# Second half of a two-layer transformer on one core: routed pass stored in tile order, rows gathered by the tokens, attention interleaved with the gathers

## The reference

```python
x = x + 0.5 * _L0_ffn_ref(_layernorm(x), ...)     # 8 experts, all computed, weighted
x = x + _L0_attn_ref(_layernorm(x), ...)          # landmark attention
x = x + 0.5 * _L0_ffn_ref(_layernorm(x), ...)
x = x + 0.5 * _L1_ffn_ref(_layernorm(x), ...)     # "first routed pass"
x = x + _L1_attn_ref(_layernorm(x), ...)          # window attention, "second attention"
x = x + 0.5 * _L1_ffn_ref(_layernorm(x), ...)     # "second routed pass"
```

```python
def _L1_ffn_ref(x, router_w, router_bias, gate_w, up_w, down_w, sgate_w, sup_w, sdown_w):
    scores = softmax(flat @ router_w.T + router_bias)          # 32 experts
    topk_scores, topk_idx = top_k(scores, 4); topk_scores /= topk_scores.sum()
    h = silu(flat @ gate_w[e].T) * (flat @ up_w[e].T)          # of the 4 chosen experts
    out = sum over the 4 of topk_scores * (h @ down_w[e].T)
    out = out + silu(flat @ sgate_w.T) * (flat @ sup_w.T) @ sdown_w.T   # shared expert
def _L1_attn_ref(x, ...):
    # q, k, v projections; 7 windows of 128 tokens, 64 apart, in each batch of 512;
    # scores/sqrt(8), softmax over the window, @ v; overlapping windows averaged; @ Wo + bo
```

## Time and profile before

| | us |
|---|---|
| three runs | 958.69, 956.48, 963.06 (median 958.69) |
| the profiled execution | 960.52 |
| its span in the trace | 959.3 |
| PE / DVE / ACT / POOL busy | 750.2 / 566.3 / 426.3 / 495.5 |
| indirect DMAs of the two tile loops on POOL (190) | 181.9 busy |
| dispatches on POOL (128) | 128.1 busy |

### The profile page before, as it was taken

How to read it: one execution, slowest core, us unless ns; L and a number is a source line. 1 busy time by engine, 2 the same in 40 slices (tenths; PEclk the granted TensorE clock), 3 DMA queues, 4 the chain that set the end, 5 groups by cost and what they waited for, 6 DMA issues and landing times.

```text
span 959.3 us, 18763 instructions
## 1 busy us (share of the span) xinstructions
PE 750.2 (78%) x6298; PEld 619.6 (65%) x6298; DVE 566.3 (59%) x1726; ACT 426.3 (44%) x1110; POOL 495.5 (52%) x488
## 2 busy tenths in 40 slices
PE   6889888999999997988977667626766896767750
PEld 5778655589777766777766656624566775666640
DVE  6975576668677588877743343318667663333325
ACT  3567646556155454555214555521532222555440
POOL 4656620036280055357753777754147770777773
PEclk9999979999799999999997999976965798999995
DMA  9999999700230050011123344333001112334316
GB/s 226 218 216 216 212 213 219 159 4 4 71 107 1 1 154 1 13 37 49 52 62 83 105 111 107 92 107 140 1 25 51 55 58 67 107 105 112 104 60 224
DMA packets 125758, 94.74 MB, mean 99 GB/s; under 512 B 10496, under 2 KB 116480, under 8 KB 125664
## 3 DMA queue, kind: packets, MB, share of 16 engines
q1 hardware_dynamic: 113472, 71.19, 32.0%
q0 software_dynamic: 10176, 21.65, 6.7%
q10 hardware_dynamic: 2016, 0.69, 0.3%
HBM read 34.12 MB, written 59.38 MB: 97 GB/s over the span
## 4 chain that ended last, share of the span: by engine, by line
PE 48%; DVE 22%; ACT 9%; POOL 9%; issue 8%; DMA 3%; SPq 1%; ACTq 0%; DVEq 0%; POOLq 0%
POOL sorted_rows L445 6%; PE banks L1625 5%; ACT y L704 5%; PE banks L793 5%; PE banks L774 4%; DVE t_low L722 3%; PE banks L1097 3%; PE banks L1654 3%; PE banks L1672 3%; PE banks L775 3%; PE banks L776 2%; ACT t_high L681 2%; PE banks L394 2%; PE banks L396 2%; PE banks L395 2%
## 5 line engine op out<-in xcount | busy, mean ns | idle before, releaser
L674 POOL DMA_INDIRECT expert_rows<-y,goal x190 | 181.9, 957 | 105.1 <-issue 60.9
L445 POOL DMA_INDIRECT sorted_rows<-rows_x,row_of x128 | 128.1, 1000 | 68.7 <-issue 36.9
L774 PE MATMUL banks<-routed_high,t_high 128*128 x192 | 60.5, 315 | 65.3 <-DVE t_low L722 65.3
L977 ACT ACTIVATE ys<-banks,wtab 128x128 f32<-128x128 f32 x256 | 73.0, 369 | 66.0 <-PE banks L1097 55.8
L774 PEld LDWEIGHTS banks<-routed_high,t_high 128*128 128x128 f32 x192 | 37.6, 196 | 76.8 <-issue 76.8
L394 PE MATMUL banks<-x_high,w_high 128*128 128x512 f32 x192 | 86.3, 450 | 0.4 <-POOL w_low L867 0.4
L739 DVE TENSOR_TENSOR h<-sg,banks 128x512 f32<-128x512 f32 x48 | 33.0, 687 | 88.8 <-ACT sg L688 88.8
L1097 PE MATMUL banks<-w,hT 128*128 128x128 f32 x512 | 72.5, 286 | 15.2 <-DVE hT L1018 14.9
L1097 PEld LDWEIGHTS banks<-w,hT 128*128 128x128 f32 x512 | 66.2, 196 | 24.1 <-DVE hT L1018 21.7
L902 POOL TENSOR_TENSOR x<-ys,x 128x512 f32<-128x512 f32 x44 | 56.3, 1280 | 46.4 <-ACT ys L977 45.8
L396 PE MATMUL banks<-x_high,w_low 128*128 128x512 f32 x192 | 77.8, 405 | 0.0
(11 more groups left out here) (297 smaller groups left out, 1911.4 us busy)
## 6 DMA issues: line engine op xcount, KB each, us to landing
sorted_rows<-zeros SPq DMA_DIRECT2D x32, 1120.0 KB, 17.3
tile<-sorted_rows SPq DMA_DIRECT2D x192, 70.0 KB
routed_low<-in_ffn_w SPq DMA_DIRECT2D x8, 512.0 KB, 3.8
w<-in_ffn_w SPq DMA_DIRECT2D x20, 192.0 KB, 4.0
expert_rows<-y,goal POOLq DMA_INDIRECT x190, 2.3
routed_down<-in_ffn_w SPq DMA_DIRECT2D x8, 256.0 KB, 5.3
sorted_rows<-rows_x,row_of POOLq DMA_INDIRECT x128
xnT<-expert_rows SPq DMA_DIRECT2D x2, 1024.0 KB, 5.7
```

Of the source, the lines that this page charges most:

```text
L445: POOL.indirect_dma_start(sorted_rows, bass.IndirectOffsetOnAxis(self.row_of[:, g, i:i + 1], 0), rows_x[:, 4 * g + i % 4, :], None).then_i ...
L674: POOL.indirect_dma_start(expert_rows, bass.IndirectOffsetOnAxis(goal[:, 4 * q + i:4 * q + i + 1], 0), y[q % 6][:, i * P:(i + 1) * P], Non ...
L774: PE.matmul(ps, t_high[q % 2][:, rows], routed.high[:, w, :].rearrange("p o c -> p (o c)"), start=True, stop=False)
L977: last = SCL.mul(ys[s % 2][:, j * P:(j + 1) * P], bank[4 + s % 2][:, j * P:(j + 1) * P], wtab[:, t, e:e + 1])
```

## The change

Three things are changed.

- In the first routed pass each tile's result is stored where the tile stands (`store`, one plain DMA per quad from SP, with ACT copying it out unweighted in one instruction), and `goals` is gone from that pass. DVE works out in four pairs of pieces (`matches`, `spots`) in which row of `expert_rows` each (token, expert) result stands. After the last store POOL gathers (`pool_gather`): 16 indirect DMAs per group, each of which brings 128 rows of 128 values to SBUF. DVE adds them, times their weight, to x (`vector_weighted`, 16 instructions of 128x128 in four dependent rounds). The loads of the kept shared weights, with their high and low parts, move into the tile loop.
- The second attention is batch by batch: rounds are numbered with a period of 15 per batch (7 with windows). The sum, norm and projection of batch b stand 7 to 2 rounds ahead of its first window, in between the routing of batch b-1. The `power` steps stand at hand-set places among POOL's gathers and dispatches.
- In both tile loops the order is changed on PE, ACT and DVE.

```diff
-        norms = [Norm(NG * n) for n in range(6)]
+        norms, last_index = [], None
+        for index in (range(0, 4), range(4, 8), range(8, 12), range(12, 16), (16, 17, 19, 21), (18, 20, 22, 23)):
+            norms.append(Norm(index, last_index))
+            last_index = index
...
+                    def store(q):
+                        SP.wait_ge(*rows_out_ready(q + 1))
+                        if q > 1:
+                            SP.wait_ge(*stored[q % 2](q // 2))
+                        SP.dma_start(expert_rows[4 * q * P:4 * (q + 1) * P, :].rearrange("(i p) d -> p i d", p=P),
+                                     y[q % 6][:, :].rearrange("p (i d) -> p i d", d=D)).then_inc(*stored[q % 2].inc)
...
+                        if gathers and q >= LAG:
+                            store(q - LAG)
...
-                    for n in range(QUADS + 1):
-                        if n < QUADS:
-                            high(n)
-                        if n > 0:
-                            evict_hT(n - 1)
-                        if n < QUADS:
-                            silu(n)
-                        if n > 0:
-                            weighted_y(n - 1)
+                    result = evict_y if gathers else weighted_y
+                    high(0)
+                    for n in range(QUADS):
+                        silu(n)
+                        if n + 1 < QUADS:
+                            high(n + 1)
+                        if n > 0:
+                            result(n - 1)
+                        evict_hT(n)
...
-                    for q in range(QUADS):
-                        low_t(q)
-                        goals(q)
-                        hidden(q)
+                    low_t(0)
+                    if not gathers:
+                        goals(0)
+                    for n in range(QUADS):
+                        hidden(n)
+                        if n + 1 < QUADS:
+                            low_t(n + 1)
+                            if not gathers:
+                                goals(n + 1)
+                        if gathers and 2 <= n < 2 + 2 * NG:
+                            if n % 2 == 0:
+                                matches(n // 2 - 1)
+                            else:
+                                spots(n // 2 - 1)
...
-                    for n in range(QUADS + 1):
-                        if n < QUADS:
-                            transposes(n)
-                        if n > 0:
-                            transposes_h(n - 1)
-                        if n < QUADS:
-                            gate_up_rows(n)
-                        if n > 0:
-                            down_rows(n - 1)
+                    transposes(0)
+                    for n in range(QUADS):
+                        gate_up_rows(n)
+                        if n + 1 < QUADS:
+                            transposes(n + 1)
+                        if n > 0:
+                            down_rows(n - 1)
+                        transposes_h(n)
+                    down_rows(QUADS - 1)
...
+            def pool_gather(self, g, home, powers):
+                if g > 1:
+                    POOL.wait_ge(*self.combined[g - 2])
+                for i in range(4 * TOPK):
+                    if i in powers:
+                        n, group = powers[i]
+                        n.power(group)
+                    POOL.indirect_dma_start(home[:, i, :], None, expert_rows[0:4 * QUADS * P, :], bass.IndirectOffsetOnAxis(row_from[:, g, i:i + 1], 0)
+                                            ).then_inc(*returned[g].inc)
+
+            def vector_weighted(self, g, home):
+                DVE.wait_ge(*self.back_here[g])
+                for n in range(TOPK):
+                    for t in range(4):
+                        xt = x[:, 4 * g + t, :]
+                        weight = rows_x[:, 4 * g + t, D + 2 * TOPK + n:D + 2 * TOPK + n + 1]
+                        last = DVE.scalar_tensor_tensor(out=xt, in0=home[:, 4 * n + t, :], scalar=weight, in1=xt, op0=ALU.mult, op1=ALU.add)
+                    if n < TOPK - 1:
+                        DV(last)
+                last.then_inc(*combined.inc)
...
+            PERIOD = NW + 8
+            ROUNDS, steps = (B - 1) * PERIOD + NW + 4, 4 * SHARED
+            BEFORE = dict(sum=7, statistics=6, normalised=5, transposes=4, copy=4, project=3, bias=2)
...
-                for i in range(SHARED):
-                    low_part(kept[i], i)
-                srt.norm.power(0)
-                for b in range(B):
-                    srt.pool_dispatch(b, 5)
+                earlier.pool_gather(0, home[0], {})
+                earlier.pool_gather(1, home[1], {7: (norm, 0)})
+                earlier.pool_gather(2, home[0], {8: (norm, 1)})
+                earlier.pool_gather(3, home[1], {0: (srt.norm, 0), 8: (norm, 2)})
+                srt.pool_dispatch(0, {4: (srt.norm, 1), 8: (norm, 3)})
+                srt.pool_dispatch(1, {3: (srt.norm, 2)})
+                srt.pool_dispatch(2, {3: (srt.norm, 3)})
+                srt.pool_dispatch(3, {})
```

More of the change, by code:

```diff
@@ L349, in build @@
         zeroed = signal("zeroed", 16)
+        stored = [signal(f"stored{p}", 16) for p in range(2)]
         def clear_sorted_rows():
@@ L398, in build, with __init__ @@
         class Sorted:
-            def __init__(self, name, scope, norm, splits, steps, ins, outs):
+            def __init__(self, name, scope, norm, splits, steps, ins, outs, gathers):
                 def own_sb(n, shape, dt=F32):
@@ new lines, in sync_engine @@
+                        if gathers and q == 3:
+                            for e, expert in enumerate(kept):
+                                SP.dma_start(expert.w[:, :, :], a["ffn1_w"][e:e + 1, :, :, :].rearrange("o p k n -> p (o k) n")
+                                             ).then_inc(*expert_loaded[0].inc)
+                        if gathers and q >= LAG:
+                            store(q - LAG)
+                    if gathers:
+                        for q in range(QUADS - LAG, QUADS):
+                            store(q)
+                    else:
+                        for p in range(6):
+                            SP.wait_ge(*returned[p](sum(tiles_of_quad(q) for q in range(p, QUADS, 6))))
+                        for g in range(NG):
+                            SP.dma_start(back[g].rearrange("p t n d -> p t (n d)"),
+                                         expert_rows[g * TOPK * GW:(g + 1) * TOPK * GW, :].rearrange("(t p n) d -> p t (n d)", p=P, n=TOPK)
+                                         ).then_inc(*back_loaded[g].inc)
@@ L1763, in scalar_engine @@
                 SCL.wait_ge(*bqs_ready(1))
[L1764 to L1770 removed]
+                norm.copy(0)
+                evict_qk(0)
                 def exp(i):
@@ L1967, in tensor_engine @@
                         srt.tensor_down(s, kept)
-            sync_engine()
             pool_engine()
```

307 lines of the change are left out of this document (178 added, 129 removed).

## The result

| | before | after |
|---|---|---|
| median | 958.89 us (956.48 to 963.06, 4 runs) | 987.12 us (986.12 to 987.88, 4 runs) |
| ratio | | 1.0289, 95% interval 1.0252 to 1.0326: slower |
| profiled execution | 960.52 us, span 959.3, clock 0.909 | 987.88 us, span 986.6, clock 0.871 |

985.5 us was forecast. The mean granted clock is lower than before (0.871 for 0.909), but that alone doesn't explain the loss: the kernel of experiment 5 has 0.876 and takes 959.10 us in its profiled execution. I read the profile after in the order of the prediction's steps.

A forecast was written before the change was run, and what follows sets the result against it. No engine is full: a PE, ACT, DVE circle bounds the tile loops, POOL close behind. 960.52 + 27.8 (attention's standing queues, net of the first loop's 26.6 gain) - 1.0 = 987.3 profiled, 985.5 us median; range 970 to 1000.

The forecast's parts named there:

- First tile loop: First routed pass: without indirect writes, quads take 3.95 us for 5.145; last `y` ends at 607.0 for 633.56.
- The circle through silu and `h`: First tile loop: gate matmul, silu, `h`, `t_low`, next gate matmul, summing to 3.95 us a quad.
- First gather: After the first tile loop: POOL waits 3.3 us for the last store, so gathers start at 610.2.
- Gathers: Ahead of and within the second attention: 64 new gathers, 1.264 us apart plus 2.25 landing, 20.2 us a group.
- the rival of 1.6: POOL's gathers before and in the attention cost 1.6 us each, +19 us, total 1004; chance 0.08.
- the cheaper gather of 1.0: Rival in the attention: gathers 1.0 us apart (-15) and shorter DVE rounds (-6), total 964 to 960; chance 0.15.
- The walk through the attention: Second attention: POOL and DVE stand for each other at `power`; the second tile loop starts 27.8 us later.
- T: Start of the gathers after the first tile loop, forecast at 610.2; attention times count from it.
- a lap: Attention on DVE: from one `power` through routing, windows, weighted sum and statistics to the next, 26.8 us.
- Second tile loop: Still has its indirect writes, so it gets POOL's pace: -1.0 us, between -2 and +1.
- That POOL would stream: Rival in the attention: the queues don't hold each other, the stage ends at 782, total 943 us; chance 0.05.
- That the first loop would stay: Rival: first tile loop keeps its pace through one SP queue or late tiles, +25 us, 1010; chance 0.07.

The follow-up runs named there:

- experiment 5: Kernel before with only the tile loops' order of operations changed, indirect writes kept: 1.0001 of the kernel before on one chip, 964.18 us (0.9952) on another.
- experiment 6: Changed kernel with its first tile loop back in the old order, plain stores and gathers kept: 1,008.47 us, 1.0411 of the kernel before.
- Experiment 2: Changed kernel with all late POOL `power` calls moved to where their sums are due: 0.9979 of the kernel before on one chip, 969.81 us (1.0020) on another.

## Why the prediction was right

**First tile loop: right, with errors that cancel.** 3.95 us a quad forecast, 4.01 measured; last `y` at 607.0, measured 607.63. Experiment 5 shows why the order alone would not have done it, and experiment 6 that the order was needed. The circle through silu and `h` holds; behind `h` it closes over PE's transposes of `h`, 0.12 us later than over the `t_low` of the forecast. The parts of the sum are further off than the sum: 21 quads save 23.9 us (108.2 to 84.3) for 25.1. The first two quads save 3.1 and the part behind the last gate matmul 0.7, together 3.8 for the estimated 1.5; the second quad, one of the two that were to stay as they are, took 7.13 us before and 4.17 now. And the loop begins 1.8 us later (507.79 for 505.99), which the forecast had not. That the rest comes to 0.7 us is luck. That POOL is a second bound close behind is shown by experiment 5: 118.8 us from first to last write for the forecast 118.8.

**First gather: right.** 610.2 forecast, 610.72 measured.

**Gathers: right.** 1.264 us forecast, 1.267 in the mean measured (1.24 to 1.38); the rival of 1.6 and the cheaper gather of 1.0 are out. DVE and POOL did not hold each other: the sum beside running gathers took 4.72 us (631.97), with POOL standing 4.66 (693.43), and the gathers beside it took 0.94 to 0.95 us, one of them 1.07. The Trainium skill, "SBUF — State Buffer", "SBUF: two separate sides", has a DVE instruction with two SBUF inputs and a GpSimd instruction that reads SBUF lock each other out for the whole instruction. Nothing of the kind is seen for this pair, the weighted sum and the issue of a gather; the measurement decides.

**The walk through the attention: right, with small errors that cancel.** Ends of `power`, forecast against measured, both from the first gather: T + 64.5 and 63.5; 91.3 and 90.0; 107.6 and 106.2; 134.4 and 133.2; 149.4 and 148.3; 175.6 and 176.3. POOL stands 16 and 20 us forecast, 15.49 and 20.89 measured; DVE 9 to 11 forecast, 8.58, 13.62 and 12.42 measured. Inside a lap the weighted sum was mis-sized, 4.7 us for 4.0: its sixteen instructions run one by one, 16 x 0.29 as in the earlier trace rows. Routing (12.5 for 12.8) and windows (6.8 for 7.3, 686.64 to 693.43) give it back, which is luck too. The stage ends at T + 216.6 for T + 215.6. Experiment 2 shows that these standing places are the cost: with them gone and nothing else changed the kernel is 20.9 us faster on B, of the 22 that it had lost there.

**Second tile loop: right.** -1.0 forecast; 119.5 us from first to last write for 121.2, -1.6 measured, and -2.0 for all that lies behind the shared steps.

**The sum.** 960.52 + 27.8 - 1.0 = 987.3 forecast, 960.52 + 29.3 - 2.0 = 987.8 measured, and 987.88 is the profiled time. Each of the two terms is within 1.5 us, and the standing places, which carry the loss, came where they were forecast. The mechanism is right; that the number is off by only 0.6 us in the profiled execution (1.6 in the median) is in part luck, since errors inside the first loop and inside the laps cancel.

**The rivals.** That POOL would stream needed a lap under 10.1 us; the lap is 26.6 (674.17 to 700.73). That the first loop would stay, and that gathers would cost 1.6, are answered above. The prediction named no rival in which the powers stand elsewhere, since the change fixes them; it is the one edit here that makes the change a draw (experiment 2, 1.0020 on B).

## What to carry to other kernels

When two in-order queues hand work to each other, the place of each small instruction among long DMAs decides, not the busy shares: POOL called three instructions of 1 us 7 to 21 us too early and three others 9 to 14 us too late for DVE, and moving these six won 21 us. Walk both queues in time, and put each such call where its operand becomes due; then look again, because every moved call shifts the next. An order that shortens the engines' circle gives some 2 us a loop and no more while a DMA queue at 1.26 us an issue is the bound 0.09 us a quad below it; take the queue's work away first, and ask where that work goes, for here the 95 indirect writes that left the loop came back as 64 gathers with little beside them.

## What the runs showed that I had not expected

**Chips differ by 14 to 16%.** The kernel before took 958.89, 968.65, 1,093.66 (1,108.08) and 1,096.64 us. The granted clock is a little lower on the slow ones (0.843 for 0.876 with the order alone), and PE's busy time 796.4 us for 755.1, but most of it is standing. Two lines of the waits of experiment 5 on chip C, and one of its timeline:

```profile
ACT sg L688 <- remote: 97.1, 16, 7.6
ACT sg L587 <- remote: 23.3, 3, 9.6
```

```profile
620.74 0.60 ACT L688 ACTIVATE sg<-banks 128x512 f32<-128x512 f32 x1 [6.67 <-remote]
```

"remote" is a release that the trace finds nowhere on this core. The matmul on which that silu waits ended at 615.2. Of the chain that ended last, 13.2% of 1,086.0 us is of this kind, 143 us; on B, for the same kernel, there is none, and its span is 128 us shorter. What holds the engines there was not found. A small change should be measured beside its own yardstick and on a chip without such waits.

**A gather costs POOL what a scatter costs.** 961 ns for the 64 gathers, 967 for the indirect writes of the same kernel, 989 for the dispatches, and 0.30 us between any two, though the gather writes SBUF and the others read it.
